# C's rows of the selective scan: from TensorE's copies to rows fetched by SyncE, with dBu in two pairs of PSUM banks

## The chip, the cores and the metric

One core of one Trainium2 chip. The metric is the device time in microseconds (us), median of the runs shown. Lower is better.

## What is computed

Four layers, each `x + layernorm(layer(layernorm(x)))`, on x of 2 x 2048 x 128 values: a time-mixing layer, a ternary feed-forward layer, a selective state-space layer (SSM), and a mixture of experts. The change is in the third. Cut to what matters:

```python
raw, gate = jnp.split(x @ W_in, 2, axis=-1)            # 128 -> 2 x 256 channels
h = jax.nn.silu(causal_conv4(raw) + conv_b)
ts, Bmat, C = jnp.split(h @ W_x, [64, 80], axis=-1)    # C, Bmat: 16 values at each time
dt = jax.nn.softplus(ts @ W_dt + b_dt)
dA = jnp.exp(dt[..., None] * -jnp.exp(A_log))          # time x 256 channels x 16 states
dBu = dt[..., None] * Bmat[:, :, None, :] * h[..., None]
state = dA * state + dBu                               # over time, for each channel and state
y = sum over the 16 states of state * C
out = ((y + h * D) * jax.nn.silu(gate)) @ W_out
```

## The kernel before, in words

The SSM stage is `phase_ssm`. The 2 x 2048 times are cut into 8 tiles (t, b) of N = 512 times: t from 0 to 3, and b, the batch row, 0 or 1. Channels lie in partitions, 256 of them as CB = 2 blocks of 128. Each tile's `body` runs over the 16 states n, so there are 128 steps in all, and each step does on each engine:

- **TensorE (PE)**: row n of B, and row n of C, are spread from one partition into all 128 by a bf16 matmul with a selector matrix. The operand `split` holds the rows in three bf16 parts that sum to the f32 value. B goes to `bcastB(n)` (L1483), after a wait for the scan of step n-2; C goes to the bank `CC` (L1486), after a wait for `c_in` of the step before. Then PE adds the products of step n-3 into `YB` by a matmul with the identity (`accumulate`, L1473).
- **VectorE (DVE)**: dBu = dtu * B for both blocks (L1761 in even steps as one instruction of 1024 elements, L1758 and L1759 in odd steps as two of 512), then two scans over time (L1746), one a block.
- **ScalarE (ACT)**: `decay`, the two exponentials for dA (L1602), and the copy of C from the bank `CC` to `csb` in SBUF (L1613).
- **GpSimd (POOL)**: the product of scan output and C for both blocks (L1694), and the last column of the scan output kept as the next tile's `carry` (L1687).

The buffers dA, hs, csb and prod have RING = 4 slots each.

DVE's PSUM tensor `DD` has three banks. Bank 0 takes block 0 of dBu in every step. Banks 1 and 2 take B in turn, and block 1 of dBu is written over B. As every step writes bank 0, dBu of step n waits for the scan of step n-1 (L1756). In odd steps the two target banks, 0 and 2, are not neighbours, so two instructions are needed. `CC` is one bank.

Into the steps are written, by hand, the preparation of the next tile (`prep`; lists such as `PE_PREP`, `ACT_PREP` say at which n each engine does which part) and the tail of the tile before (`tail`). In ACT's order the body of step n is: copy of C for n, `decay` for n+1, and then the part of `prep` or `tail` of that n. The parts that the text speaks of: at n = 8, ACT writes `split` and `rest` (the same 96 rows in f32, aliasing `sq`) and signals `whole`; at n = 9, after its product, POOL subtracts (`rest1`, L1655); at n = 10, ACT waits for that and then writes the second bf16 part (L1556) and four activations of dt (L1560, L1562); at n = 11 and 12, Exp and Ln. At n = 12 PE multiplies by `W_out` (L1454), at n = 13 ACT squares the result (L1595), at n = 14 PE takes the variance (L1459). DVE does `xn` (L1722, L1724) after step 1, `h` (L1731) after step 2, and `scaled` (L1736) after step 15. In the last tile there is no next tile to prepare. In its place is the normalisation for the next layer (`next_stage`).

SyncE (SP) loads the expert weights for the next layer into `raw` in this stage, 12 pieces of 512 KB (L1383). Pieces after the second wait for POOL's `w_low`. ACT and POOL split them at n = 2, 7 and n = 4, 8 of the first six tiles.

`keep_busy` at the start and the end of the stage issues matmuls whose results nobody reads, into `CC`.

Of the kernel before, what the change touches and what calls it, by code (L numbers as in the profile page):

```python
# [5 lines left out]
F32 = mybir.dt.float32  # L6
# [7 lines left out]
B = 2  # L14
# [20 lines left out]
for _name, _count in (  # L35
# [9 lines left out]
         "h xproj ts_in split1 whole rest1 split2 split3 dt_in magnitude expm log1p relu "  # L45
         "dt dtu bcastB bcastC dA c_in dBu scan kept prod acc y ygated "
         "down squaredC varianceC logC rstdC scaledC addedC w_in0 w_in1 w_high w_scaled w_low "
# [1244 lines left out]
def wait_past(engine, semaphore, count):  # L1292

    if not isinstance(count, int) or count > 0:
        engine.wait_ge(semaphore, count)


def phase_ssm(nc, G):
# [9 lines left out]
    with mem:  # L1308
# [26 lines left out]

        DD = mem.enter_context(nc.psum_tensor("pD3", [P, 3, N], F32))
        CC = mem.enter_context(nc.psum_tensor("pC3", [P, N], F32))
        Q = [mem.enter_context(nc.psum_tensor(f"pQ3_{i}", [P, N], F32)) for i in range(2)]
# [4 lines left out]
        def at(t, b):  # L1343
            return t * B + (b + 1)
# [4 lines left out]
        def state(t, b, n):  # L1349
            return t * (B * DST) + (b * DST + n + 1)  # L1350
# [4 lines left out]
        def slot_before(t, b, n):  # L1355
            return state(t, b, n) - RING

        def bcastB(n):
            return DD[:, 1 + n % 2, :]

        def dBu(n, c):
            return bcastB(n) if c else DD[:, 0, :]

# [12 lines left out]
        @block.sync  # L1376
        def _(sp):
            sp.dma_start(G.gatew[:, :], G.gate_w).then_inc(G.gate_loaded, 16)
            w2 = G.moe_w2.rearrange("p (e u) m -> p e (u m)", e=E // 2)
            for i in range(PIECES):  # L1380
                if i >= 2:
                    sp.wait_ge(S["w_low"], i - 1)
                sp.dma_start(raw[:, i % 2, :], G.moe_w13[:, i, :] if i < E else w2[:, i - E, :])\  # L1383
                  .then_inc(S[f"w_in{i % 2}"], 16)

        @block.tensor
        def _(pe):
# [75 lines left out]
            def keep_busy(count):  # L1463
                for _ in range(count):
                    nc.tensor.matmul(CC[:], G.sel[:, 0, :], G.sel[:, 0:4, :].rearrange("p n m -> p (n m)"),
                                     start=True, stop=True)

# [9 lines left out]
            def body(t, b):  # L1477
                for n in range(DST):

                    if n == 0:  # L1480
                        pe.wait_ge(S["split3"], at(t, b))
                    wait_past(pe, S["scan"], state(t, b, n) - 2)
                    nc.tensor.matmul(bcastB(n), G.sel[:, n, :], split[:, b, :], start=True, stop=True)\  # L1483
                      .then_inc(S["bcastB"], 1)
                    wait_past(pe, S["c_in"], state(t, b, n) - 1)
                    nc.tensor.matmul(CC[:], G.sel[:, DST + n, :], split[:, b, :],  # L1486
                                     start=True, stop=True).then_inc(S["bcastC"], 1)
                    if n < LAG and not is_first(t, b):
                        accumulate(*before(t, b), DST - LAG + n)
                    if not is_last(t, b) and n in PE_PREP:  # L1490
                        prep(*after(t, b), PE_PREP.index(n))
                    if is_last(t, b) and n < 2 * EARLY:
                        next_stage(n)
                    if not is_first(t, b) and n in PE_TAIL:
                        tail(*before(t, b), PE_TAIL.index(n))
                    if n >= LAG:
                        accumulate(t, b, n - LAG)
# [7 lines left out]
            for c in range(CB):  # L1505
                nc.tensor.matmul(YB[c][:], G.dtw[:, c * P:(c + 1) * P], tsb[:, 0, :], start=True, stop=True)\
                  .then_inc(S["dt_in"], 1)
            keep_busy(20)
            tiles(pe, body)
            pe.wait_ge(S["c_in"], NT * B * DST)  # L1510
            for n in range(DST - LAG, DST):
# [7 lines left out]
        def _(act):  # L1519
# [6 lines left out]
            def prep(t, b, step):  # L1526
# [18 lines left out]
                elif step == 5:  # L1545

                    act.wait_ge(S["xproj"], chunk(t, b, 0))
                    wait_past(act, S["bcastC"], state(t, b, 0) - 1 - DST)
                    nc.scalar.activation(split[:, b, :], Q[1][0:3 * BC, :], ACT.Copy).then_inc(S["split1"], 1)
# [21 lines left out]
            def next_stage(n):  # L1571
                i, step = divmod(n, 2)
                if step == 0:
                    act.wait_ge(S["next_centred"], i + 1)
                    if i == 0:
                        act.wait_ge(S["split3"], NT * B)
                        act.wait_ge(S["scaledC"], NT * B - 2)
                    if i >= 2:
# [10 lines left out]
            def tail(t, b, step):  # L1589
                if step == 0:  # L1590
                    if is_final(t):
                        act.wait_ge(S["next_normed"], EARLY)
                    act.wait_ge(S["split3"], prepared(t, b))
                    act.wait_ge(S["down"], at(t, b))
                    nc.scalar.activation(sq[:, b, :], Q[0][:], ACT.Square).then_inc(S["squaredC"], 1)  # L1595
                elif step == 1:
                    inverse_root(S["varianceC"], S["logC"], S["rstdC"], t, b)
# [8 lines left out]
            def body(t, b):  # L1606
                for n in range(DST):
                    if n == 0:
                        act.wait_ge(S["dt"], at(t, b))
                        decay(t, b, 0)  # L1610
                    act.wait_ge(S["bcastC"], state(t, b, n))
                    wait_past(act, S["prod"], slot_before(t, b, n))
                    nc.scalar.activation(csb[:, slot(b, n), 0, :], CC[:], ACT.Copy).then_inc(S["c_in"], 1)  # L1613
                    if n + 1 < DST:
# [36 lines left out]
        def _(pool):  # L1651
            def prep(t, b, step):
                if step == 0:
                    pool.wait_ge(S["whole"], at(t, b))
                    nc.gpsimd.tensor_tensor(rest[:, b, :], rest[:, b, :], split[:, b, :], ALU.subtract)\  # L1655
                      .then_inc(S["rest1"], 1)
# [32 lines left out]
            def body(t, b):  # L1689
                for n in range(DST):  # L1690
                    pool.wait_ge(S["scan"], state(t, b, n))
                    pool.wait_ge(S["c_in"], state(t, b, n))
                    wait_past(pool, S["acc"], slot_before(t, b, n))
# [24 lines left out]
        def _(dve):  # L1718
# [32 lines left out]
            def body(t, b):  # L1751
                for n in range(DST):
                    if n == 0:
                        dve.wait_ge(S["dtu"], at(t, b))
                    dve.wait_ge(S["bcastB"], state(t, b, n))
                    wait_past(dve, S["scan"], state(t, b, n) - 1)  # L1756
                    if n % 2:
                        nc.vector.tensor_tensor(dBu(n, 0), dtu[:, b, 0, :], bcastB(n), ALU.mult)  # L1758
                        last = nc.vector.tensor_tensor(dBu(n, 1), dtu[:, b, 1, :], bcastB(n), ALU.mult)  # L1759
                    else:  # L1760
                        last = nc.vector.tensor_tensor(DD[:, 0:CB, :], dtu[:, b, :, :],  # L1761
                                                       bcastB(n).unsqueeze(1).to_broadcast([P, CB, N]), ALU.mult)
                    last.then_inc(S["dBu"], 1)
                    scan(t, b, n)
# [20 lines left out]
            dve.wait_ge(S["whole"], 1)  # L1785
            nc.vector.tensor_tensor(rest[:, 0, :], rest[:, 0, :], split[:, 0, :], ALU.subtract).then_inc(S["rest1"], 1)
            dve.wait_ge(S["rest1"], 1)
# [791 lines left out]
```

## Time and profile before

| what | us |
|---|---|
| median of 3 runs | 1397.66 |
| lowest, highest | 1390.23, 1401.09 |
| the profiled execution's own time | 1396.73 |
| its span in the trace | 1394.7 |
| first scan of the SSM stage starts, last one starts | 506.0, 1021.4 |

The page of the profile gives each engine's busy time, the span in 40 slices, and groups of instructions by line. The views of the trace give the same by window, by line or in order of time. Busy times of neighbouring instructions on one engine can overlap a little: the next one starts before the last one's end. So the step from start to start is read from the timeline and not from the mean duration.

### The profile page before, as it was taken

How to read it: one execution, taken by the hardware profiler on the slowest of the kernel's cores; microseconds unless marked ns; L12 is line 12 of the kernel's file. 1: busy time of each engine (PE TensorE's matmuls, PEld its weight loads, DVE VectorE, ACT ScalarE, POOL GpSimd, SP SyncE). 2: the span in 40 equal slices, each digit the busy share in tenths (PEclk: the TensorE clock that was granted, in tenths of full speed). 3: DMA queues.
4: the chain of work that ended last, by engine and by line, in shares of the span. 5: the costliest groups of instructions: out<-in, count | busy, mean ns of one | idle time of the engine just before them, and what ended most of it. 6: DMA issues, size and time to landing. Idle time of an engine off the chain costs nothing. (4 is left out here: it accounts for less than half of the span.)

```text
span 1394.7 us, 16946 instructions
## 1 busy us (share of the span) xinstructions
PE 1128.6 (81%) x5010; PEld 560.5 (40%) x5010; DVE 1009.4 (72%) x1411; ACT 787.1 (56%) x1275; POOL 734.7 (53%) x617
## 2 busy tenths in 40 slices
PE   6564789999999979788888979798874688778773
PEld 2221234444444423333333333333333566566553
DVE  6996775656745369999999999999937744445445
ACT  6655545646654468586867776676723433334344
POOL 0132351423312028888879788878841565665554
PEclk8775899999999989999999999999985898899886
DMA  6000000000000001010000000000001111111115
GB/s 213 0 1 0 0 1 0 1 1 0 0 0 1 0 31 30 1 31 13 18 16 16 15 15 0 0 1 0 0 1 61 31 41 37 40 40 39 39 36 183
DMA packets 13865, 33.25 MB, mean 24 GB/s; under 512 B 3584, under 2 KB 3776, under 8 KB 13568
## 3 DMA queue, kind: packets, MB, share of 16 engines
q1 hardware_dynamic: 8368, 21.34, 4.6%
q0 software_dynamic: 4992, 10.23, 2.8%
q8 instruction: 39, 0.64, 0.2%
q10 hardware_dynamic: 432, 0.76, 0.1%
q14 instruction: 34, 0.28, 0.1%
HBM read 23.01 MB, written 9.31 MB: 23 GB/s over the span
## 5 line engine op out<-in xcount | busy, mean ns | idle before, releaser
L1694 POOL TENSOR_TENSOR prod<-hs,csb 128x1024 f32<-128x1024 f32 x128 | 301.9, 2359 | 174.0 <-DVE hs L1746 171.8
L1746 DVE TENSOR_TENSOR_SCAN hs<-dA,carry,pD 128x512 f32<-128x512 f32 x256 | 313.8, 1268 | 5.5 <-DVE pD L1761 0.8
L1473 PE MATMUL pY<-prod,const 128*128 128x512 f32 x512 | 245.8, 603 | 7.4 <-DVE h L1731 6.5
L1602 ACT ACTIVATE dA<-dt,negA 128x512 f32<-128x512 f32 x256 | 170.2, 717 | 1.4 <-DVE dt L1798 1.4
L2472 DVE SCALAR_TENSOR_TENSOR hid<-pR,silu 128x512 f32<-128x512 f32 x78 | 53.8, 690 | 135.1 <-ACT silu L2180 93.8
L1473 PEld LDWEIGHTS pY<-prod,const 128*128 128x128 f32 x512 | 96.9, 192 | 121.3 <-issue 111.2
L1613 ACT ACTIVATE csb<-pC 128x512 f32<-128x512 f32 x128 | 76.0, 594 | 88.9 <-PE pC L1486 88.8
L2180 ACT ACTIVATE silu<-pR 128x512 f32<-128x512 f32 x78 | 46.5, 596 | 133.5 <-remote 82.2
L2245 POOL DMA_INDIRECT moe_outs<-y,to x78 | 82.7, 1061 | 73.4 <-ACT y L2172 53.5
L2226 POOL DMA_INDIRECT g<-moe_rows,source x78 | 81.1, 1040 | 63.4 <-issue 31.5
L987 ACT ACTIVATE stage<-pR,vec 128x512 f32<-128x512 f32 x64 | 43.9, 688 | 100.1 <-PE pR L687 100.0
L1963 PE MATMUL pR<-x,moe_hi 128*128 128x256 f16 x312 | 91.8, 294 | 10.5 <-DVE x L2456 4.5
L1964 PE MATMUL pR<-x,moe_hi 128*128 128x256 f16 x312 | 92.0, 295 | 3.6 <-issue 3.1
L1965 PE MATMUL pR<-x,moe_lo 128*128 128x256 f16 x312 | 91.9, 295 | 1.5 <-issue 1.5
L1761 DVE TENSOR_TENSOR pD<-dtu,pD 128x1024 f32<-128x1024 f32 x64 | 78.6, 1228 | 5.5 <-PE pD L1483 0.3
L2075 PE MATMUL pY<-moe_hi,hid_hi 128*128 x312 | 64.8, 237 | 9.6 <-issue 8.9
L1403 PE MATMUL pQ<-xn,convw 128*128 128x512 f32 x112 | 59.1, 653 | 14.8 <-DVE xn L1724 14.8
L2077 PE MATMUL pY<-moe_hi,hid_lo 128*128 x312 | 64.5, 236 | 7.9 <-issue 7.9
L1486 PE MATMUL pC<-split,sel 96*128 96x512 bf16 x128 | 50.2, 393 | 24.5 <-ACT csb L1613 24.5
L2076 PE MATMUL pY<-moe_lo,hid_hi 128*128 x312 | 64.8, 237 | 6.2 <-issue 5.9
L1037 POOL TENSOR_TENSOR z_lo<-z,z_hi 128x512 f16<-128x512 f32 x8 | 10.6, 1328 | 105.0 <-DVE z_hi L1124 105.0
L429 POOL TENSOR_TENSOR o<-o,rs 128x512 f32<-128x512 f32 x8 | 12.2, 1531 | 100.9 <-DVE o L549 100.9
(424 smaller groups left out, 2756.4 us busy)
## 6 DMA issues: line engine op xcount, KB each, us to landing
raw<-moe_w SPq DMA_DIRECT2D x12, 512.0 KB, 3.7
room<-moe_outs SPq DMA_DIRECT2D x8, 512.0 KB, 7.6
hidw<-hid_w SPq DMA_DIRECT2D x1, 2048.0 KB, 10.0
moe_rows<-xt SPq DMA_DIRECT2D x8, 256.0 KB, 2.0
outT<-X SPq DMA_DIRECT2D x8, 256.0 KB, 2.0
X<-xT SPq DMA_DIRECT2D x3, 512.0 KB, 4.1
g<-moe_rows,source POOLq DMA_INDIRECT x78
moe_outs<-y,to POOLq DMA_INDIRECT x78
```

What stands on the lines that cost most here:

```text
L1473: last = nc.tensor.matmul(YB[c][:], G.ident, prod[:, slot(b, n), c, :], start=n == 0, stop=n == DST - 1)
L1602: last = nc.scalar.activation(dA[:, slot(b, n), c, :], dt[:, b, c, :], ACT.Exp, scale=negA[:, c, n:n + 1])
L1613: nc.scalar.activation(csb[:, slot(b, n), 0, :], CC[:], ACT.Copy).then_inc(S["c_in"], 1)
L1694: nc.gpsimd.tensor_tensor(prod[:, slot(b, n), :, :], hs[:, slot(b, n), :, :], csb[:, slot(b, n), :, :].to_broadcast([P, CB, N]), ALU.mult)\
L1746: last = nc.vector.tensor_tensor_scan(hs[:, slot(b, n), c, :], dA[:, slot(b, n), c, :], dBu(n, c), carry[:, b, n, c:c + 1], ALU.mult, ALU.add)
L1761: last = nc.vector.tensor_tensor(DD[:, 0:CB, :], dtu[:, b, :, :], bcastB(n).unsqueeze(1).to_broadcast([P, CB, N]), ALU.mult)
L1963: nc.tensor.matmul(out, w_hi, x_hi, start=start, stop=False)
L1964: nc.tensor.matmul(out, w_hi, x_lo, start=False, stop=False)
L1965: return nc.tensor.matmul(out, w_lo, x_hi, start=False, stop=stop)
L2075: nc.tensor.matmul(out, hid_hi[:, n % HR, at], w_hi, start=u == 0 and h == 0 and r == 0, stop=False)
L2226: nc.gpsimd.indirect_dma_start(g[:, i % GR, r, :], None, rows, bass.IndirectOffsetOnAxis(ap=source[:, 2 * i + r:2 * i + r + 1], axis=0))\
L2245: nc.gpsimd.indirect_dma_start(outs, bass.IndirectOffsetOnAxis(ap=to[:, 2 * i + r:2 * i + r + 1], axis=0), y[:, i % YR, r, :], None).then_ ...
```

## The change

C's rows no longer pass through TensorE and ScalarE. When `rest` of a tile is whole, SP writes its 16 rows of C (partitions 80 to 95, f32) to a DRAM tensor `c_rows`, and then, for each step, fetches one row of 2 KB from there into all 128 partitions of the step's slot of `csb`: 128 transfers of 256 KB, each waiting for the product that last used the slot. There is a semaphore for each slot. The loads of the weights are issued from inside the same order on SP. POOL waits for the slot's semaphore in place of `c_in`. The matmul, the copy and their waits are gone.

The bank of `CC` goes to `DD`, which now has four banks: step n uses banks 0 and 1, or 2 and 3, and B lies in the second of the pair. So dBu is one instruction of 1024 elements in each step, and it waits for the scan of step n-2 in place of n-1. The subtraction `rest1` runs on 64 partitions, so that the rows of C stay whole, and ACT waits for `c_out` (the rows have left) before it overwrites `sq`.

```diff
-        DD = mem.enter_context(nc.psum_tensor("pD3", [P, 3, N], F32))
-        CC = mem.enter_context(nc.psum_tensor("pC3", [P, N], F32))
+        DD = mem.enter_context(nc.psum_tensor("pD3", [P, 2 * CB, N], F32))
+        c_rows = nc.dram_tensor("ssm_c", (NT * B, DST, N), F32, kind="Internal").ap()
...
+        def dBu(n, c):
+            return DD[:, (n % 2) * CB + c, :]
+
         def bcastB(n):
-            return DD[:, 1 + n % 2, :]
-
-        def dBu(n, c):
-            return bcastB(n) if c else DD[:, 0, :]
+            return dBu(n, CB - 1)
+
+        def landed(t, b, n):
+            return 16 * (t * (B * DST // RING) + (b * DST + n) // RING + 1)
...
+            def rows_out(t, b):
+                sp.wait_ge(S["whole"], at(t, b))
+                sp.dma_start(c_rows[t * B + b, :, :], rest[3 * BC - DST:3 * BC, b, :]).then_inc(S["c_out"], 16)
+
+            def spread_C(t, b, n):
+                if n == 0:
+                    sp.wait_ge(S["c_out"], 16 * at(t, b))
+                wait_past(sp, S["prod"], slot_before(t, b, n))
+                sp.dma_start(csb[:, slot(b, n), 0, :], c_rows[t * B + b, n:n + 1, :].to_broadcast([P, N]))\
+                  .then_inc(S[f"c_in{n % RING}"], 16)
+
+            rows_out(0, 0)
+            for t in range(NT):
+                for b in range(B):
+                    for n in range(DST):
+                        spread_C(t, b, n)
+                        if t == 0 and b == 0 and n in (1, 2):
+                            weights(n - 1)
+                        if n in (9, 13):
+                            i = at(t, b) * 2 + (9, 13).index(n)
+                            if i < PIECES:
+                                weights(i)
+                        if n == 12 and not (t == NT - 1 and b == B - 1):
+                            rows_out(*after(t, b))
...
             def keep_busy(count):
                 for _ in range(count):
-                    nc.tensor.matmul(CC[:], G.sel[:, 0, :], G.sel[:, 0:4, :].rearrange("p n m -> p (n m)"),
-                                     start=True, stop=True)
+                    last = nc.tensor.matmul(DD[:, CB, :], G.sel[:, 0, :], G.sel[:, 0:4, :].rearrange("p n m -> p (n m)"),
+                                            start=True, stop=True)
+                return last
...
-                    wait_past(pe, S["c_in"], state(t, b, n) - 1)
-                    nc.tensor.matmul(CC[:], G.sel[:, DST + n, :], split[:, b, :],
-                                     start=True, stop=True).then_inc(S["bcastC"], 1)
...
-            pe.wait_ge(S["c_in"], NT * B * DST)
...
+                    act.wait_ge(S["c_out"], 16 * prepared(t, b))
                     act.wait_ge(S["down"], at(t, b))
...
-                    act.wait_ge(S["bcastC"], state(t, b, n))
-                    wait_past(act, S["prod"], slot_before(t, b, n))
-                    nc.scalar.activation(csb[:, slot(b, n), 0, :], CC[:], ACT.Copy).then_inc(S["c_in"], 1)
...
-                    nc.gpsimd.tensor_tensor(rest[:, b, :], rest[:, b, :], split[:, b, :], ALU.subtract)\
+                    nc.gpsimd.tensor_tensor(rest[0:2 * BC, b, :], rest[0:2 * BC, b, :], split[0:2 * BC, b, :], ALU.subtract)\
...
-                    pool.wait_ge(S["c_in"], state(t, b, n))
+                    pool.wait_ge(S[f"c_in{n % RING}"], landed(t, b, n))
...
-                    wait_past(dve, S["scan"], state(t, b, n) - 1)
-                    if n % 2:
-                        nc.vector.tensor_tensor(dBu(n, 0), dtu[:, b, 0, :], bcastB(n), ALU.mult)
-                        last = nc.vector.tensor_tensor(dBu(n, 1), dtu[:, b, 1, :], bcastB(n), ALU.mult)
-                    else:
-                        last = nc.vector.tensor_tensor(DD[:, 0:CB, :], dtu[:, b, :, :],
-                                                       bcastB(n).unsqueeze(1).to_broadcast([P, CB, N]), ALU.mult)
-                    last.then_inc(S["dBu"], 1)
+                    if is_first(t, b) and n == 1:
+                        dve.wait_ge(S["warm"], 1)
+                    wait_past(dve, S["scan"], state(t, b, n) - 2)
+                    nc.vector.tensor_tensor(DD[:, (n % 2) * CB:(n % 2) * CB + CB, :], dtu[:, b, :, :],
+                                            bcastB(n).unsqueeze(1).to_broadcast([P, CB, N]), ALU.mult)\
+                      .then_inc(S["dBu"], 1)
```

## Rows read from the trace of the kernel before

**Rows 1.** The page's slices: busy tenths of 40 equal parts of the span
```profile
DVE  6996775656745369999999999999937744445445
...
POOL 0132351423312028888879788878841565665554
PEclk8775899999999989999999999999985898899886
```

**Rows 2.** One tile's window: busy us (instructions) by engine, clock, DMA share, GB/s
```profile
697.00:761.00 64.00, 56.08 (x138) 22.73 (x138) 61.74 (x62) 47.63 (x75) 54.05 (x41) 0.97 0.06 17
```

**Rows 3.** Instructions of single lines: ns min/median/max, first and last start
```profile
L1746 DVE TENSOR_TENSOR_SCAN hs<-dA,carry,pD x256: 1253/1268/1282, 506.0 to 1021.4; 128x512 f32<-128x512 f32 x128
...
L1694 POOL TENSOR_TENSOR prod<-hs,csb x128: 2339/2358/2382, 508.5 to 1022.8; 128x1024 f32<-128x1024 f32 x128
...
L1613 ACT ACTIVATE csb<-pC x128: 577/597/607, 504.8 to 1019.1; 128x512 f32<-128x512 f32 x128
...
L1486 PE MATMUL pC<-split,sel x128: 377/378/634, 503.7 to 1018.7; 96*128 96x512 bf16 x128
...
L1473 PE MATMUL pY<-prod,const x512: 590/592/1057, 518.9 to 1026.6; 128*128 128x512 f32 x171
```

**Rows 4.** DVE's timeline: start, duration (us), line, steps 2 to 5
```profile
643.85 2.45 DVE L1746 TENSOR_TENSOR_SCAN hs<-dA,carry,pD 128x512 f32<-128x512 f32 x2 [0.19 <-DVE pD L1761]
646.22 1.38 DVE L1731 SCALAR_TENSOR_TENSOR h<-h,vec,pY 128x512 f32<-128x512 f32 x2
...
648.84 2.45 DVE L1746 TENSOR_TENSOR_SCAN hs<-dA,carry,pD 128x512 f32<-128x512 f32 x2
651.39 1.23 DVE L1761 TENSOR_TENSOR pD<-dtu,pD 128x1024 f32<-128x1024 f32 x1
652.66 2.45 DVE L1746 TENSOR_TENSOR_SCAN hs<-dA,carry,pD 128x512 f32<-128x512 f32 x2
655.22 0.70 DVE L1758 TENSOR_TENSOR pD<-dtu,pD 128x512 f32<-128x512 f32 x1
...
656.55 2.45 DVE L1746 TENSOR_TENSOR_SCAN hs<-dA,carry,pD 128x512 f32<-128x512 f32 x2
```

**Rows 5.** DVE's waits, 500 to 1030 us: total us, times, longest
```profile
DVE pD L1758 <- PE pD L1483: 10.2, 9, 2.7
...
DVE pD L1761 <- PE pD L1483: 0.3, 1, 0.3
```

**Rows 6.** Timeline, PE and DVE, around steps 12 and 13 of tile 1
```profile
616.27 0.61 PE L1486 MATMUL pC<-split,sel 96*128 96x512 bf16 x1 [2.52 <-ACT csb L1613]
616.67 3.20 PE L1454 MATMUL pQ<-ygate,ssmw 128*128 128x512 f32 x4
...
621.84 0.69 DVE L1758 TENSOR_TENSOR pD<-dtu,pD 128x512 f32<-128x512 f32 x1 [1.84 <-PE pD L1483]
```

**Rows 7.** Timeline, POOL, ACT, PE and DVE, steps 9 to 14 of tile 2
```profile
677.58 1.17 POOL L1655 TENSOR_TENSOR sq<-sq,split 96x512 f32<-96x512 f32 x1
...
678.78 0.63 ACT L1556 ACTIVATE split<-sq 64x512 bf16<-64x512 f32 x1 [3.00 <-POOL sq L1655]
...
681.60 0.59 ACT L1613 ACTIVATE csb<-pC 128x512 f32<-128x512 f32 x1
682.08 1.34 ACT L1602 ACTIVATE dA<-dt,negA 128x512 f32<-128x512 f32 x2
...
683.50 2.45 DVE L1746 TENSOR_TENSOR_SCAN hs<-dA,carry,pD 128x512 f32<-128x512 f32 x2
...
689.25 1.12 PE L1459 MATMUL pQ<-sq,const 128*128 128x512 f32 x2 [0.54 <-ACT sq L1595]
```

**Rows 8.** DMA issues: KB each, median us from issue to landing
```profile
raw<-moe_w SPq DMA_DIRECT2D x12, 512.0 KB, 3.7
...
moe_rows<-xt SPq DMA_DIRECT2D x8, 256.0 KB, 2.0
...
X<-xT SPq DMA_DIRECT2D x2, 256.0 KB, 4.1
```

**Rows 9.** Timeline, PE, end of the last tile
```profile
1013.05 2.04 PE L1459 MATMUL pQ<-sq,const 128*128 128x512 f32 x2 [3.89 <-ACT sq L1595]
...
1018.30 0.56 PE L1483 MATMUL pD<-split,sel 96*128 96x512 bf16 x1
```

More of the change, by code:

```diff
@@ L45 @@
          "h xproj ts_in split1 whole rest1 split2 split3 dt_in magnitude expm log1p relu "
-         "dt dtu bcastB bcastC dA c_in dBu scan kept prod acc y ygated "
+         "dt dtu bcastB c_out c_in0 c_in1 c_in2 c_in3 warm dA dBu scan kept prod acc y ygated "
          "down squaredC varianceC logC rstdC scaledC addedC w_in0 w_in1 w_high w_scaled w_low "
@@ L1379, in _, with weights @@
             w2 = G.moe_w2.rearrange("p (e u) m -> p e (u m)", e=E // 2)
-            for i in range(PIECES):
+            def weights(i):
                 if i >= 2:
@@ L1507, in _ @@
                   .then_inc(S["dt_in"], 1)
-            keep_busy(20)
+            keep_busy(20).then_inc(S["warm"], 1)
             tiles(pe, body)
-            pe.wait_ge(S["c_in"], NT * B * DST)
             for n in range(DST - LAG, DST):
@@ L1547, in prep @@
                     act.wait_ge(S["xproj"], chunk(t, b, 0))
-                    wait_past(act, S["bcastC"], state(t, b, 0) - 1 - DST)
+                    wait_past(act, S["bcastB"], state(t, b, 0) - 1 - DST)
                     nc.scalar.activation(split[:, b, :], Q[1][0:3 * BC, :], ACT.Copy).then_inc(S["split1"], 1)
@@ L1576, in next_stage @@
                         act.wait_ge(S["split3"], NT * B)
+                        act.wait_ge(S["c_out"], 16 * NT * B)
                         act.wait_ge(S["scaledC"], NT * B - 2)
@@ L1785, in _ @@
             dve.wait_ge(S["whole"], 1)
-            nc.vector.tensor_tensor(rest[:, 0, :], rest[:, 0, :], split[:, 0, :], ALU.subtract).then_inc(S["rest1"], 1)
+            nc.vector.tensor_tensor(rest[0:2 * BC, 0, :], rest[0:2 * BC, 0, :], split[0:2 * BC, 0, :], ALU.subtract)\
+              .then_inc(S["rest1"], 1)
             dve.wait_ge(S["rest1"], 1)
```

## The prediction, made before the changed kernel had run

> **What bounds the kernel now.** I read the page's slices first. VectorE (DVE) is at nine tenths or more in almost every slice of the SSM stage, while GpSimd (POOL) stands at seven or eight [rows 1]. The window of one tile says the same with numbers: DVE 61.7 us busy of 64, TensorE (PE) 56.1, POOL 54.1, ScalarE (ACT) 47.6 [rows 2]. The stage has 128 steps from 506.0 to 1021.4 us [rows 3], near 4.05 us each, and DVE's order of work sets the length. Then I read DVE's timeline, since busy times alone hide the gaps. In a plain even step, dBu starts at 651.39, the scans at 652.66 and the next dBu at 655.22; in the odd step dBu starts at 655.22 and the scans at 656.55 [rows 4]. So a pair of scans takes 2.55 us to the next dBu, and dBu takes 1.27 (even) or 1.33 (odd) to the scans. Last come DVE's waits: PE makes it late only 10 times, 10.5 us in all [rows 5].
>
> **dBu no longer waits for the scan just before it.** In the old order dBu(n) cannot start before the end of scan(n-1) has been signalled: 2.55 us from the first scan's start (2.56 in the other step). Where DVE's next instruction has waits that were met long ago, as `h` has, it starts 2.37 us after (643.85 to 646.22) [rows 4]. The new wait, for scan(n-2), is always met by then, and the other, for B(n), nearly always. So I take 2.37 for these steps too, 0.18 us less. Of 127 transitions from a scan to a dBu, 7 have `xn` between them, 7 `h` and 6 `scaled`; those have no gap now. The other 107 give 107 x 0.18 = 19.3 us. The bounds are 0 (the gap stays, a rival below) and 19.3, as nothing in the rows starts earlier than 2.37.
>
> This step can be set against the Trainium skill. In "VectorE: DVE Perf Modes", section "The DRAIN you can't avoid", it says that an instruction starts only when the pipeline is empty, and that "the semaphore costs nothing extra here". By that this term would be 0. The trace speaks against it, 2.37 against 2.55 us.
>
> **One dBu in place of two.** Odd steps go from 1.33 to 1.27 us from dBu to scan [rows 4]: 64 x 0.06 = 3.8 us. Their two instructions overlap, so the difference of their durations would overstate it.
>
> **C leaves PE and ACT.** 128 matmuls of 378 ns and 128 copies of 597 ns go [rows 3]. Neither engine sets the pace, so their busy time counts for nothing by itself, but they form a chain. PE may not start C(n) before ACT has copied C(n-1), ACT stands at step 10 behind POOL's subtraction, and B(n+1) is queued on PE behind C(n). In tile 1 PE stood 2.52 us for it, went on with a slower matmul (four passes in 3.20 us), and DVE waited 1.84 us at step 13 [rows 6]. Of the 10.5 us, 2.7 are the last tile's end and 0.6 the first tile's step 3, where PE waits for `xn`; both have other causes. There remain 7.2 us in 8 waits. These idle times contain the 0.10 us of the ordinary gap (the scans end 2.45 after their start, dBu starts at 2.55), which is counted above. So 7.2 - 0.8 = 6.4 us are gained; between 0, if PE is late for another reason, and 7.2.
>
> **What is late next: ACT at step 12.** Take tile 2, DVE now faster by 0.24 us a step. POOL's chain of products, weight split and subtraction at steps 8 and 9 runs without a gap and ends at 678.75 as before [rows 7]. ACT then has the second part and four activations, 2.82 us (678.78 to 681.60), and after them the exponentials for step 12, where the copy of C (0.48) stood between. They end at 681.60 + 1.34 = 682.94, against 683.42 before. The scans of step 12 started at 683.50: the slack was already only 0.08 us. Four steps after dBu(8) DVE now wants them 0.9 us earlier, at 682.6. So it waits about 0.35 us in each of the six tiles with weight splits: a loss of 2.1 us. Bounds: 0, and 0.9 x 6 = 5.4.
>
> **PE at step 14.** The square for the variance comes after ACT's chain, at about 687.9, while PE has finished its earlier work at 683.5 and has only B(14) between. It stood 0.54 us there before [rows 7]; now it stands some 4 us. Behind the variance are queued `accumulate` and B(15), for which DVE waits. With matmuls at full clock B(15) is ready near 691.0, and DVE wants it at 692.6. The last tile shows the bad case: after 3.89 us of idling, PE took from 1013.05 to 1018.30 until B(15) [rows 9], its matmuls at the lower of the two levels (1.2 in place of 2.4 GHz), as 1057 ns against 592 shows for one matmul [rows 3]. By those 5.25 us B(15) would be ready at 693.6 and DVE 1.3 us late with the signal: 6 x 1.3 = 7.8 us at worst, 0 at best. I take 3.0, as the step after 2.52 us in tile 1 was only partly slowed. In the last tile itself this chain hangs on scan 12 and not on DVE's pace; it swallows the gain of the last three steps, 0.6 us, and `xn` swallows 0.2 in the first tile.
>
> **The rows of C by DMA.** Each is 256 KB to SBUF. Other transfers of 256 KB land 2.0 or 4.1 us after the issue, and 512 KB take 3.7 [rows 8]. SP can issue row n at the end of product n-4. The product of step n starts three products later: 3 x 2.43 = 7.3 us if POOL works without a gap (2.36 for a product and the copy behind it), some 12 us at DVE's pace. So C is early with either 2.0 or 4.1, and a cost of 0 is hidden by that lead. If one source row read 128 times took over 7.3 us, POOL's busy stretches would show it first. Queued on SP are also the weights, whose wait (`w_low`) is met at steps 9 and 13, and `rows_out`, issued after product 8; it lands some 4 us later, near 677, while ACT needs it at step 13, near 687. At the start `whole` comes at 498.4; two transfers of at most 4.1 us each end before the first product, at 508.5 [rows 3]. That traffic should not slow the engines: while 12 pieces of 512 KB came in, the slowest of 256 scans took 1282 ns against a median of 1268, and the slowest product 2382 against 2358 [rows 3, 8]. The bound is 256 x 0.014 = 3.6 us; I take 0. The smaller subtraction has as many elements per partition, and `warm` is met before step 1: 0.
>
> **Sum.** 19.3 + 3.8 + 6.4 = 29.5 us won, 2.1 + 3.0 + 0.8 = 5.9 lost, 23.6 us net. The profiled execution took 1396.7 us (span 1394.7, and 2.0 around it), 0.9 below the median of the runs. I sum against it: 1396.7 - 23.6 = 1373.1, given as 1373 us, 1.8% faster.
>
> **Rivals.**
> (a) The gap stays, since a dBu that reads and writes PSUM behind a scan may need its end after all. For it: no row shows exactly this pair without a wait. Against it: `h` reads PSUM too and starts at 2.37. Then 3.8 + 6.4 = 10.2 us are won, and ACT's chain stays just in time: 1386.5 us. The Trainium skill's rule on the DRAIN ("VectorE: DVE Perf Modes") would bring this about.
> (b) The two prepared chains take more: ACT 5.4 and PE 7.8 us at their upper bounds, in place of 5.1. That is 8.1 more lost: 1381 us.
> (c) Slower: PE's clock. Per tile PE has 106 passes of 0.43 us (1.72 for four) and 16 of 0.22, 49.1 us at the full level, of 61.6 us that a tile will last. A share g of that work at the lower level takes twice its time. Up to g = 0.25 it fits in. Above g = 0.31 the tile is longer than the 64.5 us of now, and the change loses. With g = 0.4 it is 68.7 us, 8 x 4.2 = 34 us more: 1431. For it: matmuls go away that filled PE's gaps, and gaps of 2 us were followed by slow ones [rows 6]. Against it: PE's share falls only from 52.6 of 64.5 to 49.1 of 61.6, 82% to 80%, and the granted clock is 0.97 now [rows 2].
> (d) Slower: C comes late. If a row takes 4.3 us of the queue rather than its 4.1 from issue to landing, with no overlap of one transfer with the next, 128 x 4.3 = 550 us replace some 517: 1430 us. It loses from about 4.05 us per row on. Against it: 512 KB took 3.7 us.
>
> **How the numbers follow.** Forecast 0.70, (a) 0.08, (b) 0.10, (c) 0.07, (d) 0.05. About 1% (14 us) is what a measurement of this kernel can tell from no change. Faster than 1383.7 are the forecast and most of (b): 0.78. Within 1% are (a), a rest of (b) and a mild (c): 0.13. Slower: 0.09. The range goes from 1364 (no stall of ACT or PE, 1368, and some scatter of the runs, which spread by 11 us) to 1391 (rival (a) with scatter).
>
> **What would show it.** Right: the start of dBu 2.37 us after the scans in plain steps, one dBu of 1.23 us in all 128, a step of 3.63 us; DVE's waits for PE at step 13 gone; small waits of the scan for ACT's dA at step 12; transfers of C landing within 5 us and POOL waiting for DVE alone; the stage from the first scan to the last some 24 us shorter. Wrong: starts still at 2.55; POOL's product released by a DMA; DVE waiting for B at many steps with a granted clock under 0.9; longer scans or products (contention with the transfers).

## The result, and the profile after

| | before | changed |
|---|---|---|
| median of 14 runs each, same chips | 1394.55 us | 1388.13 us |
| lowest, highest | 1390.23, 1402.98 | 1381.44, 1392.94 |
| ratio of the times, 95% interval | | 0.9945 [0.9928, 0.9961] |
| profiled execution, its span | 1396.73, 1394.7 | 1392.94, 1390.9 |
| stage: first scan's start to last one's | 506.0 to 1021.4: 515.4 us | 512.0 to 1014.8: 502.8 us |

The change makes the kernel 0.55% faster, some 7.7 us. Forecast were 23.6 us and 1373, with 1364 to 1391 as range. The direction was right. The size was not: a third of it came.

The stage is the measure for what follows, as the rest of the span moves from trace to trace. In the changed kernel's trace the stage began 6.0 us later than before, though nothing ahead of it was changed. First, one line's instructions in the changed kernel, as in [rows 3]: ns min/median/max, first and last start.

```profile
L1770 DVE TENSOR_TENSOR_SCAN hs<-dA,carry,pD x256: 1252/1268/1282, 512.0 to 1014.8; 128x512 f32<-128x512 f32 x128
...
L1783 DVE TENSOR_TENSOR pD<-dtu,pD x128: 1205/1208/1230, 510.7 to 1012.4; 128x1024 f32<-128x1024 f32 x128
...
L1718 POOL TENSOR_TENSOR prod<-hs,csb x128: 2332/2356/2375, 514.5 to 1016.2; 128x1024 f32<-128x1024 f32 x128
```

The scans and the products are as long as before (medians 1268 and 2356 ns), so the 33 MB of transfers slow neither. dBu has become shorter: 1208 ns in the median against 1229 for the single dBu of the kernel before, which waited for the scan's signal. Next, DVE's timeline in the changed kernel, the answer to [rows 4 and 7].

```profile
676.92 1.21 DVE L1783 TENSOR_TENSOR pD<-dtu,pD 128x1024 f32<-128x1024 f32 x1
678.16 2.45 DVE L1770 TENSOR_TENSOR_SCAN hs<-dA,carry,pD 128x512 f32<-128x512 f32 x2
680.53 1.21 DVE L1783 TENSOR_TENSOR pD<-dtu,pD 128x1024 f32<-128x1024 f32 x1
682.38 2.45 DVE L1770 TENSOR_TENSOR_SCAN hs<-dA,carry,pD 128x512 f32<-128x512 f32 x2 [0.64 <-DVE pD L1783]
687.80 1.23 DVE L1783 TENSOR_TENSOR pD<-dtu,pD 128x1024 f32<-128x1024 f32 x1 [2.97 <-PE pD L1512]
689.07 2.45 DVE L1770 TENSOR_TENSOR_SCAN hs<-dA,carry,pD 128x512 f32<-128x512 f32 x2
```

In a plain step the scans start 1.24 us after dBu, and the next dBu 2.37 us after the scans: 3.61 us a step (676.92 to 680.53). This is what was hoped for. But at step 12 the scans wait 0.64 us, and at step 13 dBu waits 2.97 us for B. What came before on PE and ACT, in their timelines:

```profile
677.06 0.39 PE L1512 MATMUL pD<-split,sel 96*128 96x512 bf16 x1 [0.34 <-DVE hs L1770]
681.19 3.77 PE L1482 MATMUL pQ<-ygate,ssmw 128*128 128x512 f32 x4 [3.74 <-ACT dt L1587]
684.76 2.78 PE L1502 MATMUL pY<-prod,const 128*128 128x512 f32 x4
687.38 0.38 PE L1512 MATMUL pD<-split,sel 96*128 96x512 bf16 x1
```
```profile
678.14 0.63 ACT L1581 ACTIVATE split<-sq 64x512 bf16<-64x512 f32 x1 [7.41 <-POOL sq L1679]
...
680.39 0.68 ACT L1587 ACTIVATE dt<-pQ,vec 128x512 f32<-128x512 f32 x1
680.96 1.33 ACT L1629 ACTIVATE dA<-dt,negA 128x512 f32<-128x512 f32 x2
```

PE is idle for 3.74 us ahead of the product with `W_out`, which may not start before ACT's second relu (680.39) has freed its bank. Then the product takes 3.77 us and `accumulate` 2.78, where the same work takes 1.98 and 1.88 at the full level (run down13 below). The granted clock of that stretch is in the window from 681 to 688 us, after the busy times of PE, its weight loads, DVE, ACT and POOL: 0.60 of the full one.

```profile
681.00:688.00 7.00, 6.81 (x10) 2.91 (x11) 3.39 (x4) 7.00 (x12) 6.23 (x6) 0.60 0.24 85
```

Behind these passes stands B(13). PE's waits in the stage, and DVE's, the answer to [rows 5]: total us, times, longest.

```profile
PE pQ L1482 <- ACT dt L1587: 20.9, 6, 3.7
...
PE pQ L1487 <- ACT sq L1622: 4.3, 2, 4.1
```
```profile
DVE pD L1783 <- PE pD L1512: 19.4, 8, 3.3
DVE hs L1770 <- DVE pD L1783: 4.8, 10, 0.6
```

DVE waits 19.4 us for B, where it was 10.5. Six of the eight waits, 16.9 us, are at step 13 of tiles 1 to 6, with 1.7 to 3.3 us each. The 4.8 us of the scans' waits are put down to dBu, but dBu had ended; those at step 12 end with ACT's exponentials for that step (680.96 + 1.33 = 682.29, against 682.38).

The same window as in [rows 2], one tile later than the lines above: DVE is less busy in these 64 us, and the mean clock is lower (0.92 against 0.97).

```profile
697.00:761.00 64.00, 55.33 (x122) 22.32 (x122) 59.53 (x54) 39.41 (x59) 53.66 (x41) 0.92 0.28 83
```

The transfers, as in [rows 8]:

```profile
csb<-ssm_c SPq DMA_DIRECT2D x128, 256.0 KB, 3.1
raw<-moe_w SPq DMA_DIRECT2D x12, 512.0 KB, 4.8
```

**The account of the stage.** Won: 107 x 0.18 = 19.3 us for the gaps. From dBu to scan it is 1.244 us in the mean in plain steps, where it was 1.265 in even and 1.330 in odd ones, and in the 7 odd steps with another instruction ahead of dBu 1.256 in place of 1.323: 50 x 0.021 + 55 x 0.086 + 7 x 0.067 = 6.2. Lost: the waits for B, 19.4 against 9.5 (10.5 less ten ordinary gaps of 0.10): 9.9, and the scans' waits for dA, 4.8 against 1.2: 3.6. That gives 25.5 - 13.5 = 12.0 us; the stage became 12.6 us shorter.

### The profile page after: what moved, and what is told of

Same layout as the page of the kernel before. It is cut to its first block and busy times, and to the rows that moved or that the text cites. A ratio compares the mean times of both kernels' runs of the same rounds, so it can differ in the third digit from the quotient of the medians.

```text
span 1390.9 us, 16521 instructions
## 1 busy us (share of the span) xinstructions
PE 1116.7 (80%) x4882; PEld 554.9 (40%) x4882; DVE 995.4 (72%) x1347; ACT 721.3 (52%) x1147; POOL 733.8 (53%) x617
## 5 line engine op out<-in xcount | busy, mean ns | idle before, releaser
L1502 PE MATMUL pY<-prod,const 128*128 128x512 f32 x512 | 257.5, 628 | 10.3 <-DVE h L1755 8.5
L1783 DVE TENSOR_TENSOR pD<-dtu,pD 128x1024 f32<-128x1024 f32 x128 | 155.1, 1212 | 19.5 <-PE pD L1512 19.4
L1502 PEld LDWEIGHTS pY<-prod,const 128*128 128x128 f32 x512 | 101.4, 202 | 140.1 <-issue 125.0
L2100 PE MATMUL pY<-moe_hi,hid_lo 128*128 x312 | 62.8, 232 | 12.4 <-issue 12.4
L1431 PE MATMUL pQ<-xn,convw 128*128 128x512 f32 x112 | 55.2, 616 | 10.7 <-DVE xn L1748 10.7
L1512 PE MATMUL pD<-split,sel 96*128 96x512 bf16 x128 | 50.2, 392 | 16.5 <-DVE hs L1770 16.5
L1026 POOL TENSOR_TENSOR K_lo<-kstage,K_hi 128x512 f16<-128x512 f32 x24 | 28.8, 1204 | 53.7 <-DVE K_hi L1099 53.7
## 6 DMA issues: line engine op xcount, KB each, us to landing
raw<-moe_w SPq DMA_DIRECT2D x12, 512.0 KB, 4.8
room<-moe_outs SPq DMA_DIRECT2D x8, 512.0 KB, 8.0
X<-xT SPq DMA_DIRECT2D x3, 512.0 KB, 4.2
```

What stands on the lines that cost most here:

```text
L1502: last = nc.tensor.matmul(YB[c][:], G.ident, prod[:, slot(b, n), c, :], start=n == 0, stop=n == DST - 1)
L1783: nc.vector.tensor_tensor(DD[:, (n % 2) * CB:(n % 2) * CB + CB, :], dtu[:, b, :, :], bcastB(n).unsqueeze(1).to_broadcast([P, CB, N]), ALU. ...
L2100: last = nc.tensor.matmul(out, hid_lo[:, n % HR, at], w_hi, start=False, stop=u == 1 and h == 1 and r == 1)
```

## The experiments

Each run's stage is the difference of the two start times in its scans' row. The ratio is of the whole time, to the kernel before on the same chips.

| kernel | stage, us | DVE's waits for B, us | ratio [95%] |
|---|---|---|---|
| before | 515.4 | 10.5 | 1 |
| before_again | 515.2 | 10.4 | 1.001 [0.9991, 1.003] |
| changed | 502.8 | 19.4 | 0.9945 [0.9928, 0.9961] |
| after_again | 502.9 | 19.5 | 0.9956 [0.9937, 0.9974] |
| c_alone | 518.4 | 13.8 | 1.0047 [1.0028, 1.0066] |
| wait_back | 513.3 | 12.4 | 1.004 [1.0025, 1.0055] |
| down13 | 485.9 | 2.9 | 0.9819 [0.9791, 0.9846] |
| relu_first | 482.4 | 2.9 | 0.9808 [0.9778, 0.9837] |
| relu_down13 | 482.5 | 3.0 | 0.9774 [0.9748, 0.98] |
| fill12 | 488.6 | 5.3 | 0.9847 [0.9819, 0.9876] |
| relu_wait_back | 505.2 | 3.8 | 0.9938 [0.9908, 0.9968] |
| before_relu_first | 509.0 | 4.1 | 0.9981 [0.9961, 1.0001] |
| before_down13 | 509.7 | 4.8 | 0.9987 [0.997, 1.0003] |

**before_again and after_again: how steady is a trace?**

> The kernel before once more, unchanged, for a second trace. From the first scan's start to the last one's the stage took 515.4 us in the first trace. If the stage is steady, it is 515 +- 2 again, while the start of the stage (506.0 us) moves by some us from execution to execution. If instead the stage itself scatters, the 12.6 us that it got shorter in the changed kernel's trace are partly chance, and this one is off by 4 us or more.

> The changed kernel once more, unchanged, for a second trace: does its stage scatter as its 14 times (1381 to 1393) might say? If the stage is steady it is 502.8 +- 2, with waits for B of 19 +- 2 us; the scatter then lies in the stages before and behind. If it depends on where the clock falls, the waits differ by 4 us or more.

The scans' rows of the two:

```profile
L1746 DVE TENSOR_TENSOR_SCAN hs<-dA,carry,pD x256: 1252/1268/1282, 508.1 to 1023.3; 128x512 f32<-128x512 f32 x128
```
```profile
L1770 DVE TENSOR_TENSOR_SCAN hs<-dA,carry,pD x256: 1251/1268/1282, 509.1 to 1012.0; 128x512 f32<-128x512 f32 x128
```

515.2 and 502.9 us, within 0.2 of the first traces. So the stage can be compared trace by trace, to less than a microsecond here, while its start moved between 506.0 and 512.0 in all 13 traces.

**c_alone: C by transfers, dBu as before**

```diff
         def bcastB(n):
-            return dBu(n, CB - 1)
+            return DD[:, 1 + n % 2, :]
         def dBu(n, c):
-            return DD[:, (n % 2) * CB + c, :]
+            return bcastB(n) if c else DD[:, 0, :]
...
-                    wait_past(dve, S["scan"], state(t, b, n) - 2)
-                    nc.vector.tensor_tensor(DD[:, (n % 2) * CB:(n % 2) * CB + CB, :], dtu[:, b, :, :],
-                                            bcastB(n).unsqueeze(1).to_broadcast([P, CB, N]), ALU.mult)\
-                      .then_inc(S["dBu"], 1)
+                    wait_past(dve, S["scan"], state(t, b, n) - 1)
+                    if n % 2:
+                        nc.vector.tensor_tensor(dBu(n, 0), dtu[:, b, 0, :], bcastB(n), ALU.mult)
+                        last = nc.vector.tensor_tensor(dBu(n, 1), dtu[:, b, 1, :], bcastB(n), ALU.mult)
+                    else:
...
+                    last.then_inc(S["dBu"], 1)
```

> Only half of the change: C's rows come by the transfers, but dBu keeps its old banks, its wait for the scan just before and its two instructions in odd steps. Prediction's step (C's chain made PE late): DVE's waits for B fall from 10.5 us to some 4, the stage is 6 us shorter than 515.4. Theory (queue): the wait at step 12 was for relu all along, only hidden behind the wait for the copy of C; so the waits for B stay between 8 and 18 us and the stage stays at 512 to 519. Rival (contention): 128 transfers slow scans or products, whose medians of 1268 and 2358 ns rise by over 10 ns.

The stage took 518.4 us, 3.0 longer than before. The scans' row, and DVE's wait for B:

```profile
L1770 DVE TENSOR_TENSOR_SCAN hs<-dA,carry,pD x256: 1252/1268/1282, 506.8 to 1025.2; 128x512 f32<-128x512 f32 x128
```
```profile
DVE pD L1784 <- PE pD L1512: 13.8, 9, 2.8
```

Freeing PE and ACT from C, which I had down for 6.4 us, costs 3 us. The wait for C's copy had hidden the wait for relu, which now shows in PE's waits:

```profile
PE pQ L1482 <- ACT dt L1587: 18.3, 6, 3.3
```

These are steps 12 of the same six tiles. PE idles there for 2.4 to 3.3 us, against 1.9 to 2.5 before, as without C's matmuls it comes to the product earlier (in tile 2 it is through with B(12) at 678.79, against 680.12). In tile 2 the product then takes 3.43 us in place of 1.95. The scans' median is unchanged: no contention.

**wait_back: the wait for scan n-1 put back into the changed kernel**

```diff
-                    wait_past(dve, S["scan"], state(t, b, n) - 2)
+                    wait_past(dve, S["scan"], state(t, b, n) - 1)
```

> The changed kernel, with pairs of banks and one dBu a step, but the wait for the scan of step n-1 put back. Theory: a dBu starts 2.55 us after the scans again, not 2.37; where the stall at step 13 pins the time (5 steps in each of 6 tiles) nothing is lost, so the stage is 10 to 16 us longer than 502.8. If the signal costs nothing, as the Trainium skill's rule on the DRAIN has it, the start stays where it is and the stage too.

The stage took 513.3 us, 10.5 longer than the changed kernel's, at the low end of what was expected. DVE's timeline:

```profile
648.76 2.45 DVE L1770 TENSOR_TENSOR_SCAN hs<-dA,carry,pD 128x512 f32<-128x512 f32 x2
651.32 1.23 DVE L1783 TENSOR_TENSOR pD<-dtu,pD 128x1024 f32<-128x1024 f32 x1
652.58 2.45 DVE L1770 TENSOR_TENSOR_SCAN hs<-dA,carry,pD 128x512 f32<-128x512 f32 x2
```

2.56 us from the scans to dBu again. So the wait for a signal that has only just been given costs 0.18 to 0.19 us. In total this kernel is 0.4% slower than the one before, though its stage is 2.1 us shorter; more on that below.

**down13: the product with W_out one step later**

```diff
-            PE_PREP, PE_TAIL = (0, 1, 2, 3, 4, 5, 6, 8, 9, 10), (12, 14)
+            PE_PREP, PE_TAIL = (0, 1, 2, 3, 4, 5, 6, 8, 9, 10), (13, 14)
```

> The changed kernel with one edit: the product with W_out goes from PE's step 12 to step 13, so that B(13) is no longer queued behind a matmul that waits for ACT's relu. Theory (queue): DVE's waits of 2.9 to 3.3 us for B at step 13 go, its waits for B fall from 19.4 us to under 6, and the stage gets 10 to 18 us shorter than the 502.8 of the changed kernel. Rival (clock): PE stands idle for ACT wherever the product is placed, comes back at the lower clock, and the same 2 to 3 us a tile turn up at B(14) or B(15): waits stay over 12 us and the stage within 4 us.

The stage took 485.9 us, 16.9 less than the changed kernel's. PE's timeline in tile 2, and DVE's waits:

```profile
668.84 0.39 PE L1512 MATMUL pD<-split,sel 96*128 96x512 bf16 x1 [0.33 <-DVE hs L1770]
669.07 1.88 PE L1502 MATMUL pY<-prod,const 128*128 128x512 f32 x4
672.46 0.39 PE L1512 MATMUL pD<-split,sel 96*128 96x512 bf16 x1 [1.50 <-DVE hs L1770]
672.99 1.98 PE L1482 MATMUL pQ<-ygate,ssmw 128*128 128x512 f32 x4
...
678.96 1.12 PE L1487 MATMUL pQ<-sq,const 128*128 128x512 f32 x2 [1.89 <-ACT sq L1622]
```
```profile
DVE hs L1770 <- DVE pD L1783: 4.8, 10, 0.7
...
DVE pD L1783 <- PE pD L1512: 2.9, 3, 2.0
```

By 672.99 relu is done, PE has worked in between, and the product takes 1.98 us. The queue theory's numbers came, but PE also idled less, so this run doesn't tell queue from clock. The waits at step 14 are real now (1.89 us here), without delaying DVE.

**fill12: PE kept busy, queue unchanged**

```diff
+                    if n == 12 and not is_last(t, b):
+                        for _ in range(11):
+                            nc.tensor.matmul(bcastB(n), G.sel[:, n, :], split[:, b, :], start=True, stop=True)
                     nc.tensor.matmul(bcastB(n), G.sel[:, n, :], split[:, b, :], start=True, stop=True)\
```

> The changed kernel, where PE at step 12 of all tiles but the last repeats the matmul of B(12) 11 times before the one that signals (some 2.4 us, into a bank that nobody reads yet), so that it idles some 1.3 instead of 3.7 us before the product with W_out, which still waits for relu and still stands in front of B(13). Theory (clock): the 3 us that DVE waits at step 13 are the four product passes and the four of accumulate at the lower clock (3.6 + 2.6 us, against 3.4 at the full one); they fall from 3.77 us for the product to about 1.9 and DVE's waits for B from 19.4 us to under 8, the stage to 486 to 494. Rival (queue): the wait for relu alone makes B(13) late; the waits stay over 14 us and the stage over 499.

The stage took 488.6 us, and the waits for B at step 13 fell to 0.24 to 0.32 us in five tiles and to none in the sixth. PE's timeline, and the DVE row that answers to 687.80 above:

```profile
670.44 2.55 PE L1514 MATMUL pD<-split,sel 96*128 96x512 bf16 x11 [0.33 <-DVE hs L1773]
672.82 0.38 PE L1515 MATMUL pD<-split,sel 96*128 96x512 bf16 x1
674.58 1.98 PE L1482 MATMUL pQ<-ygate,ssmw 128*128 128x512 f32 x4 [1.38 <-ACT dt L1590]
676.39 1.88 PE L1502 MATMUL pY<-prod,const 128*128 128x512 f32 x4
678.11 0.38 PE L1515 MATMUL pD<-split,sel 96*128 96x512 bf16 x1
```
```profile
678.53 1.23 DVE L1786 TENSOR_TENSOR pD<-dtu,pD 128x1024 f32<-128x1024 f32 x1 [0.32 <-PE pD L1515]
```

The product still waits for relu and still stands in front of B(13). Only the idle time before it is 1.38 us in place of 3.74, and it now takes 1.98 us in place of 3.77. The granted clock of this stretch is the full one:

```profile
674.50:679.00 4.50, 4.42 (x11) 2.10 (x12) 3.53 (x4) 4.50 (x7) 3.72 (x4) 1.00 0.42 117
```

So of the 2.97 us in tile 2, 2.65 are the lower clock and 0.32 the queue by itself. The rival (queue alone) falls. The queue is still needed for the loss, as down13 showed: it puts B(13) behind the slow passes. 14 us of stage came back through matmuls that compute nothing.

**relu_first: ACT's four activations ahead of the one that waits for POOL**

```diff
+                    for c in range(CB):
+                        act.wait_ge(S["dt_in"], chunk(t, b, c))
+                        wait_past(act, S["dBu"], state(t, b, 0) - 1 - DST)
+                        nc.scalar.activation(dtu[:, b, c, :], Q[c][:], ACT.Abs, bias=col("b_dt", c))\
+                          .then_inc(S["magnitude"], 1)
+                        nc.scalar.activation(dt[:, b, c, :], Q[c][:], ACT.Relu, bias=col("b_dt", c))\
+                          .then_inc(S["relu"], 1)
                     act.wait_ge(S["rest1"], at(t, b))
                     nc.scalar.activation(split[0:2 * BC, b, :], rest[0:2 * BC, b, :], ACT.Copy).then_inc(S["split2"], 1)
-                    for c in range(CB):
...
```

> The changed kernel with one edit on ACT: at step 10 the four activations of dt come before the one that waits for POOL's subtraction, as they don't need it; PE's order is as in the changed kernel. Theory (PE's product at step 12 waits for relu, and relu stands behind the subtraction): PE's 20.9 us of waiting for relu fall to under 2, DVE's waits for B from 19.4 to under 6, and the scans' wait for dA at step 12 (4.8 us with all others) to under 3; the stage takes 480 to 490 us. Rival: what counts is only where the product stands (as in the run with it at step 13); B(13) is still queued behind it and late by over 1 us a tile, stage over 494.

The stage took 482.4 us, 20.4 less than the changed kernel's. PE no longer waits for relu at step 12, and the scans' waits fell from 4.8 to 1.2 us. DVE's waits:

```profile
DVE pD L1783 <- PE pD L1512: 2.9, 3, 2.0
DVE hs L1770 <- DVE pD L1783: 1.2, 4, 0.5
```

**relu_down13: both repairs**

> Both repairs on the changed kernel: the activations of dt first and the product with W_out at step 13. If they cure the same wait, the second adds nothing: stage 481 to 484, time within 3 us of either alone (1368). If each had a part of its own, the stage is under 480.

The stage took 482.5 us. The second repair adds nothing to the first, so for B they cure the same wait; the 3.5 us by which relu_first is ahead of down13 are the scans' waits for dA (4.8 against 1.2 us), which only relu_first cures. The ratios of the two kernels with it, 0.9774 and 0.9808, overlap. They have the shortest stages of the study.

**relu_wait_back: the gap without a stall to hide in**

> The changed kernel with ACT's four activations first (stage 482.4 us) and the wait for the scan of step n-1 put back. With no stall to hide it, the gap shows whole: 107 starts later by 0.18 us, stage 482.4 + 19 = 499 to 503. If part of it was hidden by something else too, as 12.6 of 29.5 us were in the changed kernel, the stage is under 496.

The stage took 505.2 us, 22.8 more than relu_first, and slightly above the 503 expected. The later dBu also lengthens the way to the scans, by 0.02 us: a plain step takes 3.82 us in place of 3.61, and 107 x 0.21 = 22.5. In the changed kernel the same wait was worth 10.5 us; the other 12 were eaten by the stall. Of these some 10 can be seen: with the wait put back, DVE's waits for B fell from 19.4 to 12.4 us and the scans' for dA from 4.8 to 1.6.

**before_relu_first and before_down13: the repairs without the change**

> The same edit of ACT's order in the kernel before. There PE waited at step 12 for the copy of C(11), which on ACT stands behind the four activations and these behind the subtraction. The copy at step 11 stays behind the activation that waits for the subtraction, so PE still waits, but some 2.3 us shorter a tile. Expected: DVE's waits for B 10.5 us to 3 to 5, stage 508 to 512. If the wait at step 12 had nothing to do with ACT's order, the stage stays at 515.

> The product with W_out at step 13 in the kernel before. Theory: C(12) waits for the copy of C(11) in front of B(13) there in any case, so moving the product takes only its own 1.7 us out of the way: the waits for B fall from 10.5 us by 5 to 8, the stage is 509 to 513. If the edit is worth the same 17 us in either kernel, the stage is under 502 and the change itself has nothing to do with what the edit freed.

Stages of 509.0 and 509.7 us, 6.4 and 5.7 less than before. So the kernel before had the same fault, at a third of its price. In total neither is clear of no change (0.9981 and 0.9987, both intervals reach 1). The rows of DVE's waits in before_relu_first:

```profile
DVE pD L1758 <- PE pD L1483: 3.7, 4, 2.2
...
DVE pD L1761 <- PE pD L1483: 0.4, 2, 0.3
```

With the repair in both, the change is worth 509.0 - 482.4 = 26.6 us of stage, and 0.9981 against 0.9808, some 24 us, in total. Without it, 12.6 of stage and 7.7 in total.

## Why the prediction was wrong

**The gap and the single dBu: right.** The start moved from 2.55 to 2.37 us as read from `h` [rows 4], and 22.8 us of stage hang on that wait when nothing hides it. The Trainium skill's sentence in "VectorE: DVE Perf Modes", "The DRAIN you can't avoid", that the semaphore costs nothing extra, does not hold for this pair of instructions: the measurement decides. The same section also says "A next op that is not held starts earlier", which the prediction left out, and with that the 2.37 us agree. The single dBu was undersized: 6.2 us in place of 3.8, as the way from dBu to the scans gets shorter by 0.02 us in even steps too.

**"C leaves PE and ACT", 6.4 us: this step failed.** I read PE's 2.52 us at C [rows 6] as the price of the chain through C's copy, and took it away with C. But the product with `W_out`, next on PE, has a wait of its own for relu (in `tail`, step 0), and ACT's relu stands directly in front of that copy. These are the lines of tile 2 in the kernel before, ACT's and PE's:

```profile
681.03 0.68 ACT L1562 ACTIVATE dt<-pQ,vec 128x512 f32<-128x512 f32 x1
```
```profile
682.24 0.39 PE L1486 MATMUL pC<-split,sel 96*128 96x512 bf16 x1 [2.12 <-ACT csb L1613]
```

Relu ends at 681.71 and the copy at 682.19 [rows 7], 0.48 us later. The wait was covered, not caused, by C: c_alone shows 13.8 us of waits for B, where 10.5 - 6.4 = 4.1 should have been left. Of the eight waits that I had put down to C, six are these at step 13. The two others, 0.8 us together in the first tile, are gone in c_alone. I had listed what is queued behind the waiting instruction, but not looked at whether the next one would have waited just as long.

**"PE at step 14", 3.0 us: the right mechanism in the wrong place.** Idling, then the lower clock, then B late is exactly what took the gain, but at step 12, in six tiles, with 1.7 to 3.3 us each in DVE's waits. I had reckoned PE free from 683.5 on and the only long idle at step 14; in fact PE came to step 14 late and did not wait there (only 4.3 us in 2 waits, 4.1 of them in the last tile). With the stall repaired the idle at step 14 appears (1.89 us in down13) and costs nothing. The change itself lengthened the idling at step 12, as PE arrives at the product earlier: in tile 2 it idles 2.12 us in the kernel before, 3.25 with C gone (c_alone) and 3.74 with the faster DVE too.

**ACT at step 12, 2.1 us: right, but too small.** The scans' waits for dA cost 3.6 us more than before, 0.49 to 0.64 a tile at step 12 in place of the 0.35 predicted.

**The transfers, 0: right.** A row lands 3.1 us after its issue, between the 2.0 and 4.1 of [rows 8], and POOL's products never wait for a transfer. The weights land later (4.8 against 3.7 us), and nobody waits for them.

**Of the rivals,** (b) had the right ingredients, at step 14 in place of 12, and the right sign; its 1381 is still 7 us short. In (c) I asked whether the whole tile would become PE's; a mean clock of 0.92 against 0.97 hides that slow passes fell between a wait and B(13), where DVE pays for them.

**From the stage to the total.** The stage gave 12.6 us and the total 7.7 (a ratio times the median of before, set against the stage's difference). In all edited kernels the total moved less favourably than the stage, by 1.2 to 7.7 us, with intervals of about 2 to 4 us each way. The 13 traces, one for each row of the table, point behind the stage. From the last scan's start to the end of the span it is 373.0 to 376.1 us in the nine traces with C by transfers, 374.7 in the mean, and 367.2 to 373.4 in the four without, 370.6 in the mean. Ahead of the stage there is no such difference (508.4 and 508.8 us in the mean). As the four scatter by 6 us, this is a pointer and no proof. Of these 4 us some 1.9 lie between the last scan's start and the next layer's gate product: 21.6 us in both traces of the kernel before and 23.4 in both of the changed kernel, where the last tile's product and the next layer's first matmul took 3.61 us each, in place of 2.61 and 1.96. But before_down13 has 23.4 too, so that this part comes with the change is not shown. Why the part behind the stage is longer stays open; no run here was made to separate it.

## What to carry to other kernels

Before a wait is booked as a gain, delete it on paper and ask what the next instruction in that queue would wait for; if that ends within a fraction of a microsecond of the old wait, nothing is won. When the engine that sets the pace gets faster, the others can idle longer at fixed waits, and here TensorE came back from such idling with matmuls at the lower clock; so look for work with a critical result queued just behind them. Order the instructions of a helper engine so that those which wait for nothing stand ahead of the one that waits for a slow neighbour: here one moved loop was worth more on top of the change than the change by itself, 20 us of stage against 13, and 6 without the change.

## What the runs showed of the hardware

- Of TensorE's clock: after 3.74 us of idling, eight passes took 3.77 and 2.78 us; after 1.38 us, with 2.55 us of useless matmuls ahead, they took 1.98 and 1.88. The granted clock was 0.60 from 681 to 688 us in the first case and 1.00 in the second, so the slow passes ran mostly at the lower of the two levels (1.2 and 2.4 GHz). The idle time just before does not decide by itself: in the kernel before the product took 1.95 us behind 2.12 us of idling (tile 2) and 3.36 us behind 1.88 (tile 6). Matmuls that nobody reads gained 14 us of stage.
- A DVE instruction whose waits were met long ago starts 0.18 us earlier behind a scan than one that waits for that scan's signal (2.37 against 2.55 us), and a dBu so started is 21 ns shorter (1208 against 1229).
- One row of 2 KB in DRAM, fetched into 128 partitions (256 KB), lands after 3.1 us in the median, 7.5 at most, beside 2.0 us for another transfer of 256 KB in this kernel. 128 of them in 500 us slowed no scan and no product.
